# TensorE's order in a long cross attention: key tiles taken two by two, with one block of full-array work per pair

## What is computed

```python
q = (x_query @ Wq.T).reshape(B, T_q, h, d).transpose(0, 2, 1, 3)
k = (x_kv @ Wk.T).reshape(B, T_k, h, d).transpose(0, 2, 1, 3)     # T_k = 1500
v = (x_kv @ Wv.T).reshape(B, T_k, h, d).transpose(0, 2, 1, 3)
q = _rope(q, T_q)
k = _rope(k, T_k)
attn = jnp.einsum('bhqd,bhkd->bhqk', q, k) * SCALE
attn = jax.nn.softmax(attn, axis=-1)
out = jnp.einsum('bhqk,bhkd->bhqd', attn, v)
return out.transpose(0, 2, 1, 3).reshape(B, T_q, DIM) @ Wo.T
```

## Time and profile before

| what | value |
|---|---|
| median of 3 runs | 1459.55 us (1456.22 to 1461.99) |
| profiled execution: span from first to last instruction | 1397.8 us |
| time around the span (median less span) | 61.8 us |
| matmuls of the scores, first to last | 605.8 to 1293.7 us of the span |
| TensorE busy in the span | 1277.9 us (91%) |
| VectorE, ScalarE, GpSimd busy in the span | 76%, 57%, 60% |

### The profile page before, as it was taken

One profiled execution on the slowest core, in us unless ns is written; L12 is line 12 of the kernel. 1 busy time (PEld: TensorE's weight loads), 2 busy tenths in 40 slices (PEclk: granted clock), 3 DMA queues, 4 the chain that ended last, 5 costly groups with the idle time before them and its releaser, 6 DMA issues.

```text
span 1397.8 us, 42378 instructions
## 1 busy us (share of the span) xinstructions
PE 1277.9 (91%) x17390; PEld 904.3 (65%) x17390; DVE 1066.3 (76%) x1817; ACT 802.5 (57%) x1760; POOL 842.5 (60%) x839
## 2 busy tenths in 40 slices
PE   6878999998997898678999999999999999988998
PEld 4556888788984666345565666656656666565986
DVE  6895676766677888777888888888888887886556
ACT  2542335336662333147677777777777777777541
POOL 6676232161567566578677786776777767665033
PEclk9887999999998999879999999999999999999999
DMA  5002700004521504546765465565565654546112
GB/s 139 2 1 68 244 3 2 2 28 131 163 59 29 78 12 89 104 133 134 156 136 145 118 129 134 113 139 130 112 145 133 114 139 96 120 85 186 43 49 54
DMA packets 84849, 136.19 MB, mean 97 GB/s; under 512 B 19809, under 2 KB 68322, under 8 KB 81314
## 3 DMA queue, kind: packets, MB, share of 16 engines
q1 hardware_dynamic: 80946, 125.87, 38.7%
q0 software_dynamic: 3712, 7.61, 1.9%
HBM read 98.38 MB, written 40.76 MB: 100 GB/s over the span
## 4 chain that ended last, share of the span: by engine, by line
PE 44%; ACT 6%; DVE 3%; issue 2%; POOL 2%; DMA 1%; ACTq 0%; POOLq 0%; SPq 0%; DVEq 0%
PE ps L2024 9%; PE ps L2040 8%; PE ps L1986 6%; PE ps L1977 6%; PE ps L2000 4%; ACT ARENA L2196 3%; ACT ARENA L2180 2%; PE ps L2502 2%; PE ps L2466 2%; DVE ARENA L2117 2%; PE ps L2513 1%; PE ps L2049 1%; PE ps L2476 1%; POOL ARENA L2245 1%; DMA key_parts<-ARENA 1%
## 5 line engine op out<-in xcount | busy, mean ns | idle before, releaser
L2117 DVE TENSOR_REDUCE ARENA<-ps 112x2 f32<-112x1000 f32 x384 | 456.3, 1197 | 109.7 <-PE ps L2000 108.0
L2196 ACT ACTIVATE ARENA<-ps 125x448 f32<-125x448 f32 x768 | 375.8, 546 | 106.5 <-PE ps L2024 103.7
L2245 POOL TENSOR_TENSOR ARENA<-ARENA 64x500 f32<-64x500 f32 x192 | 219.9, 1145 | 33.5 <-ACT ARENA L2174 9.1
L2024 PEld LDWEIGHTS ps<-ARENA 64*125 64x125 bf16 x3072 | 123.2, 134 | 143.3 <-ACT ARENA L2196 98.4
L2040 PE MATMUL ps<-ARENA 125*17 125x112 f32 x6144 | 210.3, 263 | 0.0
L2024 PE MATMUL ps<-ARENA 64*125 64x112 bf16 x3072 | 167.5, 228 | 28.7 <-ACT ARENA L2196 24.8
L2040 PEld LDWEIGHTS ps<-ARENA 125*17 125x17 f32 x6144 | 129.4, 97 | 57.3 <-issue 48.0
L2000 PE MATMUL ps<-ARENA 64*112 64x500 bf16 x768 | 153.7, 385 | 9.8 <-DVE ARENA L2117 8.9
L130 POOL TENSOR_TENSOR rs<-rs,mhalf 128x1 f32<-128x1 f32 x96 | 73.0, 762 | 122.4 <-DVE rs L125 122.1
L2251 POOL TENSOR_TENSOR ARENA<-ARENA 128x500 f32<-128x500 f32 x96 | 136.8, 1425 | 7.5
L2256 POOL TENSOR_TENSOR ARENA<-ARENA 128x500 bf16<-128x500 f32 x96 | 104.1, 1085 | 57.4 <-ACT ARENA L2180 57.4
(11 more groups left out here) (332 smaller groups left out, 2401.7 us busy)
## 6 DMA issues: line engine op xcount, KB each, us to landing
ARENA<-key_parts SPq DMA_DIRECT2D x192, 187.5 KB, 4.9
ARENA<-in_ctxT SPq DMA_DIRECT2D x96, 250.0 KB, 3.2
key_parts<-ARENA SPq DMA_DIRECT2D x64, 375.0 KB, 3.9
slots<-in_c_blank SPq DMA_DIRECT2D x2, 1472.0 KB, 12.8
results<-ARENA SPq DMA_DIRECT2D x42, 64.0 KB, 2.7
last_slots<-in_c_blank SPq DMA_DIRECT2D x1, 2144.0 KB, 12.5
ARENA<-in_L_ffn_W SPq DMA_DIRECT2D x1, 2048.0 KB, 8.5
ARENA<-in_L_ffn_W SPq DMA_DIRECT2D x4, 512.0 KB, 10.6
```

The costliest lines, as they stand in the source:

```text
L2024: m = e.matmul(ps[0:KT, b1[h], 112 * g:112 * g + 112], KS[b % 4][r, g, KT * kt:KT * kt + KT], Q1[r, b % 2, 112 * g:112 * g + 112], start=T ...
L2117: e.tensor_reduce(mxp[0:112, b % 2, 2 * g:2 * g + 2, ch], ps[0:112, b1:b1 + 2, 0:500], AX, ALU.max) \
L2196: e.activation(Pb[0:KT, n % NP_, 448 * h:448 * h + 448], ps[0:KT, b1[h], 0:448], ACT.Exp, bias=0.0, scale=1.0).then_inc(exped.sem, 1)
L2245: e.tensor_tensor(T2[r:r + 64, :], T0[64 - r:128 - r, n % 2, :], sin[64 - r:128 - r, sl], ALU.mult) \
```

## The change

Only `order()` changes (and a tuple of step names is added). Before, the loop ran over single tiles: a score and a peak, then, behind every odd tile, the two applies with the short steps between them, and the keys or values steps behind whichever tile they belong to. Now the loop runs over pairs of tiles m and m + 1: score and peak of m, score and peak of m + 1, then all single-bank steps of both tiles in one block (VISIT), then the two applies, then `own`. What does not use TensorE keeps its place among the tiles, apart from standing ahead of the applies.

```diff
+            VISIT = ("keys", "values", "full", "fold", "turn", "out", "finish", "query", "route", "count", "turn_slots")
...
-                for n in range(B * NK + 2):
-                    b, kt = divmod(n, NK)
-                    if n < B * NK:
+                for m in range(0, B * NK + 2, 2):
+                    visit = []
+                    for n in (m, m + 1) if m < B * NK else ():
+                        b, kt = divmod(n, NK)
                         yield ("score", b, kt)
                         if kt < 6 and b + 1 < B:
                             yield ("peak", b + 1, 6 + kt)
                         if kt >= 6 and b + 2 < B:
                             yield ("peak", b + 2, kt - 6)
-                    steps = side(b)[kt] if n < B * NK else []
-                    short = [x for x in steps if kt % 2 and x[0] in ("full", "fold", "turn", "out", "finish", "query")]
-                    if n >= 3 and n % 2:
-                        yield ("apply", *divmod(n - 3, NK))
-                        yield from short
-                        yield ("apply", *divmod(n - 2, NK))
-                        if kt == 1:
-                            yield ("own", b - 1)
-                    singles = [x for x in steps if x[0] in ("keys", "values")]
-                    yield from singles
-                    yield from [x for x in steps if x not in short and x not in singles]
-                    if n == B * NK:
+                        steps = side(b)[kt]
+                        visit += [x for x in steps if x[0] in VISIT]
+                        if n % 2:
+                            yield from visit
+                        yield from [x for x in steps if x[0] not in VISIT]
+                    if m >= 2:
+                        yield ("apply", *divmod(m - 2, NK))
+                        yield ("apply", *divmod(m - 1, NK))
+                        if m % NK == 0:
+                            yield ("own", m // NK - 1)
+                    if m == B * NK:
                         yield ("begin", 0)
```

## The result

| | before | after |
|---|---|---|
| median of 4 runs each | 1457.88 us | 1503.67 us (1498.48 to 1506.34) |
| ratio | | 1.0319, 95% interval 1.0286 to 1.0353 |
| profiled execution: span, time | see below | 1503.3, 1505.11 us |

The changed kernel is slower by 3.2%, 46 us.

A forecast was written before the change was run, and what follows sets the result against it. The prediction took TensorE to bound the stage: new waits less savings gave +0.289 us a round, +49.7 over 172 rounds, less 1.0 and 2.0, so 1459.55 + 46.7 = 1506.3 us, 3.2% slower; range 1490 to 1533.

The forecast's parts named there:

- The wait: TensorE's second score of a round waits for the first bank's exponential: score spacing 0.58 becomes 1.22, 0.64 us new per round.
- What covers the other waits: Visit, next round's first score, applies and other engines: no further wait, cost nothing; margin at the visit's first step 0.15 us.
- second rival, A second wait: ScalarE's exponentials start 0.5 us later in half the rounds, so second score and visit wait: +43 us more, 1549; chance 8%.
- The savings by touching: On TensorE, two full-array blocks that touch in the visit save 0.17 us; eight pairs in 12 rounds, 1.36 us.
- The sum: Attention stage: twelve rounds 46.40 us against 42.93, +0.289 a round; 172 rounds +49.7, less 1.0 and 2.0, +46.7 us.
- Fewer changes of mode win: TensorE's second score need not wait, so a round takes 0.58 there: −0.351 us a round, 1396 us; chance 5%.
- Hidden: Most of the second score's wait is hidden or was there before: no change to +1.5%; chance 4%.
- The clock: TensorE's clock, held to be no rival: full clock (1.00) at 84% busy in an earlier stretch; new rounds have 83%.
- The profiled span: Whole profiled execution: 1397.8 + 46.7 = 1444.5 us, with the median taken to lie 61.75 above the span.
- What was to be seen: Profile after: second score idle 0.5 to 0.6 us, 1.2 after the first; TensorE 80 to 86% busy; batch 23.2 against 21.5.

The follow-up runs named there:

- second trace of before: The kernel before, unchanged, profiled once more: span 1456.4 us against 1397.8 in its first trace; median 1455.03 us, ratio 1.0002.

## Why the prediction was right, point by point

**The wait.** Idle 0.57 before the second score and 1.22 from score to score were read off the one place in the trace of before that already had the order, and both came to the hundredth in 106 of the 128 rounds from 700 to 1200 us. Over the whole span TensorE's waits for the exponential rose from 27.8 us in 54 to 106.1 us in 180; the prediction had 172 new ones and ten old, 182. The Trainium skill, page "TensorEngine Tiling (Array Packing)", section "Restrictions and Gotchas" (PSUM Pressure), says that row tiling presses on PSUM because row tiles write to different banks; the 71.7 us of waits for a bank in 500 us agree.

**What covers the other waits.** The view lists no wait of the visit, a peak or the applies from 700 to 1200 us. ACT's copy of bank 3, which the prediction had named under its second rival as "at a batch's end, bank 3 right ahead of the next exponentials", costs nothing either: in the round that follows a batch's last applies it runs ahead of the exponentials (at 963.92 in the batch shown), and the second score waits 0.51 there and comes 1.16 behind the first (963.73 to 964.89). In one batch of 22 it waits 0.76 (at 941.55); why that one differs I have no row for.

**The savings by touching** were half right. Two applies in a row take 0.89 in every round, as priced. A short step behind values or keys saves about 0.10: values ahead of a fold take 0.98 (945.89 to 946.87) and keys ahead of `full` 0.95 (953.92 to 954.87). The further 0.07 that the earlier trace rows have on the second block is there for `finish` (0.20 against 0.26 in the trace of before, which the prediction took as 0.30) and `out` (0.31 against 0.42), but not for fold (0.53 against 0.56) and `full` (0.29 against 0.30), and keys ahead of `turn` save nothing, 1.03. So 0.17 a pair was too much: it was a row of two long blocks, put on pairs of a long and a short one. This step failed in its size.

**The sum** came out in part by luck. Twelve rounds were to take 46.40 and take 46.78 (959.97 to 1006.75). The 0.38 more are 0.34 in the two rounds with `turn`, 0.13 in those with `full` and 0.09 in those with a fold, less 0.12 for the rounds behind a batch's last applies and 0.06 for `finish` and `out`. With the 42.80 of the second trace of before a round is longer by 0.332, where the prediction had 0.289. At 0.332 its 172 rounds would have lost 57 us, not 49.7. But the loss is not in 172 rounds. At the `turn` that ends the fifth batch the changed kernel is still 4.3 us ahead (747.95 against 752.29), about as it was at the first score; at the one that ends the 28th it is 42.3 behind (1292.03 against 1249.70). So 46.7 us are lost in 138 rounds, 0.338 each (the two ends, in the second trace of before and in after):

```profile
752.29 0.26 PE L2055 MATMUL ps<-ident,ARENA 56*128 56x56 f32 x1
...
1249.70 0.27 PE L2055 MATMUL ps<-ident,ARENA 56*128 56x56 f32 x1
```
```profile
747.95 0.27 PE L2057 MATMUL ps<-ident,ARENA 56*128 56x56 f32 x1
...
1292.03 0.27 PE L2057 MATMUL ps<-ident,ARENA 56*128 56x56 f32 x1
```

The 30 rounds before show no loss; the one stop of the second trace of before (2.4 us at 727.83) lies there and can hide some 4 us. The last 24 rounds, where the clock falls and both kernels stand still at times (below), add 1.8. The rate was put too low and the number of rounds that pay too high, and the two errors nearly cancel: 46.7 forecast, 45.8 measured. The sum takes off 3 us and its lower bound 5, without a reason given.

**The rivals.** *Fewer changes of mode win* fell: the changes do cost (0.10 here and there), but the second score would have had to come at 0.58. *A second wait* did not come: the view lists none in 128 rounds, and the second score waits longer than 0.57 in one of them. *Hidden* fell with 128 waits in 128 rounds. The clock was no rival: 1.00 from 700 to 1200 us at 86% busy.

**The profiled span.** The prediction took 61.75 us as the time that lies around the span. In all the other profiled runs it is 1.8; by that the rest was one quick execution. It did no harm as the sum is a difference, put on the median. But the absolute span it named for after, 1444.5, was wrong by 59.

**What was to be seen.** Idle 0.5 to 0.6, spacing 1.2, share 80 to 86%, clock, visit without waits: all as said. The share is 86% and not the 83% worked out, since a round idles 0.57 and not the 0.64 by which it was to grow there. Two batches took 46.78 for 46.4. That the last 18 tiles are no longer than before can't be judged: from the first to the last start of their scores they take 23.9 us after (1360.0 to 1383.9), but 19.9 and 24.5 in the two traces of before.

## What to carry to other kernels

Where blocks take turns in a small ring of banks, the time from one use of a bank to the next is a latency that does not depend on the work between (here 0.53 to the reader's start, 0.55 of reading, 0.14 to hand it back; 1.22 with one peak between or two); long work that needs another bank belongs into that gap, and gathering it elsewhere to spare changes of mode costs 0.57 to win 0.1. A new order can be there already at some edge of the old one, as here, at a start or an end: look there for its price before estimating it. And take a second trace of the same program before explaining where an absolute number goes.

## What the runs showed that was not expected

Two executions of one program differed by 58.6 us of span, though two batches in the stage's middle took 42.93 and 42.80 us. Some of this kind of loss can be seen in after near the stage's end, where TensorE stands still for an exponential whose engine itself had come to a halt (TensorE, then ScalarE):

```profile
1326.64 0.68 PE L2026 MATMUL ps<-ARENA 64*125 64x112 bf16 x8 [4.13 <-ACT ARENA L2198]
```
```profile
1325.70 0.35 ACT L2210 COPY ARENA<-ps 128x224 f32<-128x224 f32 x1 [5.34 <-remote]
```

The 5.34 us are put down to no engine of the core. DVE stops at the same time, for 5.31 us, while GpSimd issues indirect transfers; the granted clock from 1300 to 1350 us is 0.86. The second trace of before has stops of up to 1.33 us put down to "issue" in its last batches and a clock of 0.83 there; the first, quick one has 0.93 from 1250 to 1300 us, where its stage ended. What stops the engines, perhaps the supply of instructions, was not tried and stays open.
